# A retention and mixture-of-experts block: the loop written out, row-tiled scores and state, routing weights widened by DMA

## What is computed

```
x = x + attn(layernorm(x));  x = x + ffn(layernorm(x))
attn: q, k = rotary(x Wq, x Wk);  scores = (q k^T) * decay_mask (causal, gamma_h^(t-s));  o = scores v
      o_n = o * rsqrt(mean(o^2)) * g_norm_w;   out = (o_n * silu(x Wg)) Wo
ffn:  comb = top-2 weights of softmax(x gate_w), renormalized
      h_e = silu(x up_w[e] + up_b[e]);  y = sum_e comb_e * (h_e down_w[e] + down_b[e]) + shared expert
```

## Time and profile before

| | |
|---|---|
| Median of 3 runs | 172.55 us (172.54 to 173.57) |
| Profiled execution | 173.23 us, of which span 171.5 us |
| PE busy | 157.3 us (92%) |
| DVE busy | 122.6 us (71%) |
| ACT busy | 82.1 us (48%) |
| POOL busy | 52.9 us (31%) |

### The profile page before, as it was taken

How to read it: one execution, slowest core, us unless ns; L and a number is a source line. 1 busy time by engine, 2 the same in 40 slices (tenths; PEclk the granted TensorE clock), 3 DMA queues, 4 the chain that set the end, 5 groups by cost and what they waited for, 6 DMA issues and landing times.

```text
span 171.5 us, 3275 instructions
## 1 busy us (share of the span) xinstructions
PE 157.3 (92%) x1072; PEld 112.7 (66%) x1072; DVE 122.6 (71%) x350; ACT 82.1 (48%) x155; POOL 52.9 (31%) x73
## 2 busy tenths in 40 slices
PE   6499988989899999999999999999999999999981
PEld 6399665848668777556877865666678656564430
DVE  3759899798898988773789977865678665744411
ACT  3142772334399535232697617024897522973110
POOL 8799418460633340400060611100606111000000
PEclk9999999999999999999999999999999999999999
DMA  4960000000000000000100000000200000010002
GB/s 156 332 214 0 0 4 2 4 0 0 0 6 2 2 0 4 0 0 4 33 28 0 0 0 0 0 0 0 61 2 0 4 0 0 0 48 15 0 0 61
DMA packets 5568, 4.21 MB, mean 25 GB/s; under 512 B 794, under 2 KB 5172, under 8 KB 5556
## 3 DMA queue, kind: packets, MB, share of 16 engines
q1 hardware_dynamic: 5140, 3.53, 6.9%
q10 hardware_dynamic: 416, 0.52, 0.8%
HBM read 3.01 MB, written 1.05 MB: 24 GB/s over the span
## 4 chain that ended last, share of the span: by engine, by line
PE 71%; DVE 14%; issue 6%; POOL 3%; ACT 3%; DMA 2%; DVEq 0%; POOLq 0%; ACTq 0%
PE bY L1192 17%; PE bS L1072 6%; PE bC L1179 5%; PE bU L250 5%; PE bU L252 4%; PE bU L251 4%; PE bV L1131 4%; PE bO L1108 3%; PE bY L996 2%; DVE XN L664 2%; PE bO L1102 2%; PE bV L1122 2%; PE bV L250 2%; PE bX L1053 2%; DMA X<-x 2%
## 5 line engine op out<-in xcount | busy, mean ns | idle before, releaser
L1192 PE MATMUL bY<-HG,DW 128*128 128x512 f32 x64 | 31.6, 593 | 0.0
L356 POOL TENSOR_TENSOR RR<-MS,NHALF 128x8 f32<-128x8 f32 x8 | 13.6, 1700 | 56.5 <-DVE MS L735 56.5
L502 ACT ACTIVATE HB<-bU,UB 128x512 f32<-128x512 f32 x36 | 24.4, 690 | 13.2 <-PE bU L252 12.7
L832 DVE TENSOR_TENSOR HG<-bC,HB 128x512 f32<-128x512 f32 x32 | 22.1, 691 | 11.7 <-PE bC L1179 9.3
L250 PE MATMUL bU<-XH,UWH 128*128 128x512 f32 x36 | 18.9, 524 | 0.1
L1179 PE MATMUL bC<-CT,SEL 128*128 128x512 f32 x32 | 16.9, 529 | 1.1 <-DVE HG L832 1.0
L1072 PE MATMUL bS<-QBD,KT 128*128 128x512 f32 x28 | 14.7, 608 | 1.1 <-DVE S L726 0.6
L1192 PEld LDWEIGHTS bY<-HG,DW 128*128 128x128 f32 x64 | 11.6, 190 | 5.2 <-issue 3.8
L375 POOL TENSOR_TENSOR RS<-VE,NHALF 128x2 f32<-128x2 f32 x8 | 6.0, 746 | 28.8 <-DVE VE L764 28.7
L252 PE MATMUL bU<-XH,UWL 128*128 128x512 f32 x36 | 14.2, 395 | 0.0
L251 PE MATMUL bU<-XL,UWH 128*128 128x512 f32 x36 | 14.1, 392 | 0.0
(11 more groups left out here) (151 smaller groups left out, 351.8 us busy)
## 6 DMA issues: line engine op xcount, KB each, us to landing
out<-OUT SPq DMA_DIRECT2D x8, 128.0 KB, 1.9
X<-x SPq DMA_DIRECT2D x7, 128.0 KB, 4.9
UW<-upw SPq DMA_DIRECT2D x1, 576.0 KB, 5.8
DW<-dnw SPq DMA_DIRECT2D x1, 576.0 KB, 6.3
W<-wqkvg ACTq DMA_DIRECT2D x1, 384.0 KB, 4.0
CN<-const SPq DMA_DIRECT2D x1, 228.5 KB, 3.3
X<-x ACTq DMA_DIRECT2D x1, 128.0 KB, 2.8
WO<-wot SPq DMA_DIRECT2D x1, 128.0 KB, 6.0
```

The source lines that it names most:

```text
L356: pool.tensor_tensor(RR[:, p], MS[:, p], NHALF[:, 0:2 * H], ALU.pow).then_inc(rr.sem, 1)
L502: act.activation(HB[:, k, :], bU[k % 2][:, :], ACT.Silu, bias=UB[:, e:e + 1]).then_inc(hid.sem, 1)
L832: dve.tensor_tensor(HG[:, k % RING, :], bC[:, :], HB[:, k, :], ALU.mult).then_inc(gated.sem, 1)
L1192: pe.matmul(bY[:, :], DW[:, w], HB[:, 0, :] if k == 0 else HG[:, k % RING, :], start=(k == 0), stop=(k == E)).then_inc(down.sem, 1)
```

## The change

- **Order.** The loop is gone; every step of the four groups is written out, and each engine has an order of its own. PE's order also has explicit waits (`after(signal, ...)`) where a bank must be free. The groups' attention runs further ahead of the experts: the first up projection comes after the scores of pair (1, 1) and after the projections of group 2's first pair.
- **Scores and state.** Queries and keys are copied once, to QKT. Scores are 8 matmuls for a pair, each on 32 rows (one head) and 128 columns, each head into its own bank of bA (four banks). S holds only the 32 x 64 block of each head, one head in each strip of 32 partitions; attend's state part is 8 matmuls of 32 rows and 64 columns, the update one DVE instruction. masked works on a pair with two instructions of 512 elements, as before one for each tile.
- **Banks.** q/k, v, gates and the transposed q/k have one bank of bA each; x1_t, state_add, out_t, proj_out, x2_t, router and comb_t share the bank bM.
- **Routing weights.** For groups 0 to 2 the 8 rows of comb go from a copy in SBUF (CR) to a scratch in memory, and four DMAs (two experts each) write them to all partitions (CB); gating reads CB. The last group keeps spread_comb, now into two banks of bA in turn.
- **Moved.** Normalizing (from group 1 on, and all of the second layernorm) from DVE to ACT with a bias computed on DVE; eps additions, the low parts of the expert weights, the output norm's folding and the selector's copy from DVE to POOL. Rotary tables are loaded (4 x 512 KB) instead of built on POOL. keep_x1 is gone, the sum is written to X itself. keep_busy counts 23 instead of 30.
- **Routing.** Ranks are taken on logits, and the softmax's division is left to the last renormalization.

```diff
-            def scores(g, m):
...
-                pe.matmul(score_bank(g, m)[:, :], KT[:, p, b, :], QBD[:, p, b].rearrange("r h n -> r (h n)"), start=True,
-                          stop=True).then_inc(sc_ps.sem, 1)
+            def scores(g, p):
+                pe.wait_ge(qkt.sem, qkt.at(g, p))
                 for b in range(2):
                     for h in range(H):
                         r = slice(h * DK, (h + 1) * DK)
+                        last = pe.matmul(bA[:, h, b * P:(b + 1) * P], QKT[r, p, 1, b, :], QKT[r, p, 0, b, :], start=True,
+                                         stop=True)
+                last.then_inc(sc_ps.sem, 1)
...
+            def attend(g, p):
...
-                        pe.matmul(bO[:, b * HV:(b + 1) * HV], QT[:, p, b, :], S[:, p, b, :], start=(b == 0), stop=False)
+                            pe.matmul(bA[:, h, b * DV:(b + 1) * DV], QKT[r, p, 0, b, :], S[r, n % 4, b * DV:(b + 1) * DV],
+                                      start=(b == 0), stop=False)
...
-                pe.matmul(bC[:, :], SEL[:, expert(k), :], CT[:, :], start=True, stop=True).then_inc(spread.sem, 1)
+                if k <= 2:
+                    pe.wait_ge(ogr.sem, ogr.at(LAST, 1))
                 else:
+                    pe.wait_ge(gated.sem, gated.at(LAST, k - 3))
+                pe.matmul(bA[:, k % 2, :], SEL[0:EX0, expert(k), :], CT[0:EX0, LAST % 2, :], start=True,
+                          stop=True).then_inc(spread.sem, 1)
...
+            def widen(g):
+
+                sp.wait_ge(cr_sb.sem, cr_sb.at(g))
+                sp.dma_start(scratch[g], CR[EX0:EX0 + E, :]).then_inc(sent.sem, 16)
+                sp.wait_ge(sent.sem, 16 * (g + 1))
+                for j in range(E // 2):
+                    if g:
+                        sp.wait_ge(gated.sem, gated.at(g - 1, 2 * j + 1))
+                    src = scratch[g, 2 * j:2 * j + 2, :].unsqueeze(0).to_broadcast([P, 2, GC])
+                    sp.dma_start(CB[:, 2 * j:2 * j + 2, :], src).then_inc(wide[j].sem, 16)
...
             def gating(g, k):
+                if g == LAST:
+                    dve.wait_ge(spread.sem, k)
+                    src = bA[:, k % 2, :]
+                else:
+                    if k % 2:
+                        dve.wait_ge(wide[(k - 1) // 2].sem, 16 * (g + 1))
+                    src = CB[:, k - 1, :]
...
-                for h in range(H):
-                    r, c = slice(h * DK, (h + 1) * DK), slice(h * DV, (h + 1) * DV)
-                    last = dve.scalar_tensor_tensor(
...
+                dve.scalar_tensor_tensor(out=S[:, (n + 1) % 4], in0=S[:, n % 4], scalar=CN[:, GCH0:GCH0 + 1],
+                                         in1=bM[:, 0:2 * DV], op0=ALU.mult, op1=ALU.add).then_inc(st.sem, 1)
...
             keep_busy(10)
             x1_t(0)
-            keep_busy(4)
+            keep_busy(8)
             proj_qk(0, 0)
-            keep_busy(8)
+            proj_g(0, 0)
+            proj_qk(0, 1)
             proj_v(0, 0)
+            after(xl1, 0)
+            x1_t(1)
+            proj_v(0, 1)
```

More of the change, by code:

```diff
@@ L1212, in _ @@
             scores(0, 0)
[L1213 to L1224 removed]
+            after(xl1, 1)
+            state_add(0, 0)
+            keep_busy(3)
+            attend(0, 0)
+            after(st, 0, 0)
+            state_add(0, 1)
@@ L1375, in _ @@
-            y_t(g)
+            after(x1, 0, 0)
+            state_add(1, 0)
+            after(ogr, 0, 1)
+            scores(1, 0)
+            after(st, 1, 0)
+            x2_t(0, 0)
+            attend(1, 0)
+            after(xl2, 0, 0)
+            out_t(0, 1)
+            proj_out(0, 1)
+            after(ogr, 1, 0)
+            proj_qk(2, 0)
+            after(ogr, 1, 0)
+            proj_v(1, 1)
+            after(ogr, 1, 0)
+            proj_g(1, 1)
+            after(ogr, 1, 0)
+            qk_t(1, 1)
@@ new lines, in _ @@
+            scores(1, 1)
+            up_proj(0, 0)
+            after(ogt, 1, 0)
+            x1_t(3)
+            up_proj(0, 1)
+            attend(1, 1)
+            after(xl1, 3)
+            state_add(2, 0)
+            up_proj(0, 2)
+            after(st, 2, 0)
+            router(0)
+            up_proj(0, 3)
+            after(ogr, 1, 1)
+            scores(2, 0)
+            up_proj(0, 4)
+            after(route_a_step, 0, 0)
+            proj_out(1, 0)
+            up_proj(0, 5)
+            down_proj(0, 0)
@@ new lines, in _ @@
+            after(x1, 1, 0)
+            out_t(1, 1)
+            attend(2, 0)
+            proj_out(1, 1)
+            up_proj(0, 6)
+            up_proj(0, 7)
+            after(x1, 1, 1)
+            x2_t(1, 0)
+            after(ogr, 2, 0)
+            proj_v(2, 1)
+            after(ogr, 2, 0)
+            proj_g(2, 1)
+            after(ogr, 2, 0)
+            proj_qk(3, 0)
+            after(xl2, 1, 0)
+            comb_t(0)
+            up_proj(0, 8)
+            after(ogr, 2, 0)
+            qk_t(2, 1)
@@ new lines, in _ @@
+            y_t(0)
+            up_proj(1, 6)
+            after(v_sb, 3, 1)
+            after(sg, 3, 1)
+            scores(3, 1)
+            after(x1, 2, 1)
+            out_t(3, 0)
+            up_proj(1, 7)
+            down_proj(1, 0)
+            after(ogt, 3, 0)
+            state_add(3, 0)
+            down_proj(1, 1)
+            after(st, 3, 0)
+            x2_t(2, 1)
+            attend(3, 1)
+            down_proj(1, 2)
+            after(xl2, 2, 1)
+            router(2)
+            down_proj(1, 3)
```

1636 lines of the change are left out of this document (815 added, 821 removed).

## The result

The changed kernel takes **154.01 us** (median of 4 runs, 153.01 to 155.38), against 172.56 us for the kernel before; the ratio is 0.8898, 95% interval 0.8854 to 0.8943. 156 was predicted, with 150 to 166 as the range. A few executions, such as the one of 155.38 here and two of the four of wide_moved, ran in a slower state at a lower granted clock; medians and ranges count them, ratios do not.

The account below looks back on a forecast made before the run. The prediction took a VectorE-set lead, then TensorE's instruction stream, as the bound. Lead 48.5, filled part 103.3 and end 3.5 sum to a 155.3 us span; with 1.05 added, 156.3, say 156 us, range 150 to 166.

Parts of the forecast that it names:

- Lead: Start to first up projection: first projection at 11.45, 31 us of VectorE work, 6 idle; 48.5 us against 47.87 before.
- Scores' packs: A pair's eight score matmuls on row tiles: 0.5 us instead of 1.72, saving 1.22 a pair, 2.44 a group.
- State's packs: A pair's eight state matmuls in attend, on row tiles: 0.45 us instead of 0.86, saving 0.82 a group.
- The row shows none of a cost: TensorE, state matmuls to half-width ones: changing tile shape priced at nothing, against some tenths of a microsecond a pair by rule.
- Spreads: 24 of 32 routing-weight spreads leave TensorE at 0.23 us each: 1.84 us saved a group, for three groups.
- Widening: DMAs spreading routing weights between comb_t and gating: first takes 3.6 us including start, with 4.9 us left for it.
- Gating from SBUF: Gating on VectorE with two SBUF inputs: 0.708 us against 0.691 before, so nothing gained there.
- Filled part: First up projection to last sum: 93.9 us of TensorE work times a factor of 1.10, 103.3 us.
- Tiles without overlap: Rival for score and state matmuls: row tiles do not overlap, 172.6 us, or 164 at half overlap; chance 0.12.
- Clock in the lead: Rival: TensorE at half rate through the lead's middle, +5 us, 161, or the whole lead, +10, 166; chance 0.10.
- Shared banks: Rival: shared banks stall the filled part, factor 1.2 instead of 1.1, 9.4 us more, 166; chance 0.08.
- Late weights: Rival: widened weights reach gating late, 160 us, or 194 at 60 GB/s; chance 0.08, 0.03 of it slower than before.

Follow-up runs that it names:

- wide_moved: Kernel before plus only the DMA widening of routing weights, with VectorE's statistics, rotation and normalization of a token pair moved ahead of gated products 1 and 2; 180.82 us.
- pool_order: Changed kernel with GpSimd's selector moved behind the fourth group's deviation and the first attention output's normalization; 152.91 us, ratio 0.8866.
- full_scores: Changed kernel with each score matmul contracting all 128 rows instead of its head's 32; 162.15 us, ratio 0.9382.
- spread_time: Changed kernel with 24 512-column float32r matmuls put back on TensorE, one for each spread taken away; 157.62 us, ratio 0.9097.
- wide_late: Changed kernel with each group's widening DMAs held back by two 576 KB loads on the same queue; 177.89 us, ratio 1.0284.
- before_wide: Kernel before with only the DMA widening of routing weights added and 24 spreads gone, in its own orders; 190.38 us, ratio 1.1014.
- full_state: Changed kernel with attend's state matmuls contracting all 128 rows instead of 32; 166.26 us, ratio 0.9609.
- norm2_dve: Changed kernel with the second normalization back from ScalarE to VectorE; 153.39 us, ratio 0.8903.
- both: Changed kernel with the edits of norm2_dve and pool_order together; 153.92 us, ratio 0.8931.
- less_busy: Changed kernel without the 13 filler matmuls behind the first transposes and in the lead, the first ten kept; 156.2 us, ratio 0.8992.

## Why the prediction was right, step by step

The mechanism is the predicted one: row tiles overlap, TensorE's own work bounds the filled part, and the span is 3.3 us under the 155.3 that was summed. Of the signs that were named, "DVE near 103 us", the first up projection near 48.5 and no stretch at 0.21 behind 20 us came; records 23 to 35 ns apart did not (38 and 41), and a gated product did wait for CB, twice, 1.5 us in all.

- **Lead.** 48.5 predicted, 48.42 measured; that they agree so closely is luck. Its terms erred in both directions: VectorE was busy 29.4 us in it, not 31, and stood 7.5, not 6. And the first projection, taken over at 11.45, comes at 11.4 or at 10.2 from one execution to another (pool_order).
- **Scores' packs.** 0.5 predicted between the bounds 0.37 and 1.76; 0.66. **State's packs:** 0.45 predicted; 0.60. The direction was right (full_scores: 111 ns a record against 41), the terms were 0.15 too small: four row tiles overlap less well than the column tiles they were priced by (23 ns). The gain of a pack in scores is 1.06, not 1.22, and 0.86 where the way back costs 0.2.
- **"The row shows none of a cost" for changing the tile shape: wrong.** The step looked at one row, from the state matmuls to the half-width ones. The rows where it shows are the full-width matmuls behind narrow tiles, 0.43 instead of 0.23 in the chain above, and with full_scores it is gone. The kernel before had them too, behind state_add (four transposes in 0.65 instead of 0.44 us, at 45.72). The rule of the Trainium skill (TensorEngine Tiling (Array Packing), section Tiling Modes), that a change of the mode drains the engine, agrees with these rows.
- **Spreads.** 1.84 a group predicted; in spread_time two thirds of such work came back as time.
- **Widening.** 3.6 us for the first transfer predicted; 4.1 to 8.1 us from issue to landing, the median 6.3, and slices of up to 357 GB/s, so every partition reading the same rows is no slower than the loads. The gate waited 1.5 us in all, as said hidden. But its price as a rival was far too low. It was given "a few late microseconds ... (160)"; wide_late shows 24 us for 7 us of delay a group, and before_wide 18 us slower than before with no delay at all. The prediction priced a late transfer by the down projection that needs it and did not ask what stands behind the waiting gate in VectorE's queue. What made the widening nearly free (0.8 us) was the other part of the change, the order, as far as wide_moved shows it.
- **Gating from SBUF.** 0.708 predicted for two SBUF inputs; 0.683, no difference from a bank. The 0.708 of the earlier trace rows is a mean with one long instruction in it (0.831 us, the median is 0.688).
- **Filled part.** 93.9 x 1.10 = 103.3 predicted; 100.1, a factor of 1.07 as in the kernel before. The work was 93.9 + 4 x 0.16 + 5 x 0.15 for the packs + some 4 x 0.2 for the scores' returns = 96.1, and TensorE stood 1.3 us up to 145. The remaining 2.7 us were not traced step by step; the 0.34 behind the router is one of them. The expected growth of the factor by shared banks did not come: the 3 us by which the prediction was too high lie here. The same sum says what the gain is made of: TensorE's work in this part fell from 112.4 to 96.1 us, 16.3, while the part itself fell by 20.1. The other 3.8 us are waits and lengthened steps that are gone. They go with the new orders and banks; no run has these alone, so that share is argued, not shown.
- **End.** 3.5 predicted and measured. **VectorE** 103 predicted, 101.0; **ScalarE** about 80, 84.1.
- **The rivals.** Tiles without overlap: refuted by full_scores. Clock in the lead: behind 12 us it did not fall in the changed kernel's two profiles, but in full_state, norm2_dve and both it did, at 35 to 47 us, and less_busy has it up to 15.6 us. This rival was near: full_state's gaps are the changed kernel's own, norm2_dve has one of 1.6 instead of 1.1 us. From the first projection to the first up projection these kernels take 1.9 (less_busy), 2.2 (both) and 3.0 us (norm2_dve) more, and full_state 6.9, of which its two longer packs at full rate are 2.3. So the fall cost some 2 to 4.6 us where 5 was the price. Shared banks: no sign. Late weights: not here, and dearer than priced.

## What to carry to other kernels

A wait for a DMA on an in-order engine costs what is queued behind it, on that engine and on those that wait for that work, and behind all six stalls of TensorE of about 5 us (before_wide, wide_late) a stretch at half rate followed, behind those of about 3 us (wide_moved) in two of three. So move a transfer under cover together with the order around the wait: the same widening lost 18 us in the old order, 6 with a few steps of that order moved, and 0.8 us in the new kernel. Thin contractions gained by row tiles: eight float32 matmuls of 32 rows (16 records) took 0.66 us instead of 1.78 on all rows, and up to 0.2 us went to the way back to full width. And look at more than one profile of a kernel before a microsecond is put down to an edit.

## What the hardware showed that was not expected

VectorE instructions with two tensors in SBUF, and GpSimd's multiply OG (two tensors in SBUF too), exclude each other in this trace. Timelines of both engines in the changed kernel, VectorE first:

```profile
25.56 1.58 DVE L666 TENSOR_TENSOR QKR<-RA,RB 128x512 f32<-128x512 f32 x1
```
```profile
84.22 0.68 DVE L795 TENSOR_TENSOR HG<-CB,HB 128x512 f32<-128x512 f32 x1
84.82 1.00 DVE L724 SCALAR_TENSOR_TENSOR NM<-MV,RS 128x2 f32<-128x2 f32 x1
```
```profile
25.55 1.04 POOL L323 TENSOR_TENSOR OG<-OGR,RR 128x512 f32<-128x512 f32 x1
```
```profile
84.21 1.59 POOL L323 TENSOR_TENSOR OG<-OGR,RR 128x512 f32<-128x512 f32 x1
```

At 25.6 us OG had begun first, keeps its 1.04, and QKR, usually 0.68, ends 0.55 us behind it. At 84.2 it is the reverse: the gated product keeps its 0.68, OG takes 1.59 instead of 1.04 and ends 0.9 later, and NM behind it, two numbers a partition and usually 0.16, takes 1.00 and ends with OG. Products that read a bank kept their time beside an OG (RA at 91.07 took 0.69). In all there are five such meetings in the trace (25.6, 43.2, 65.5, 84.2 and 105.3 us), which lengthen six instructions by 0.55 to 0.9 us each. It is read from the trace alone; no run was made for it. The Trainium skill (SBUF — State Buffer, section SBUF: two separate sides) states that the two engines share a pair of ports under an exclusive lock, held for a whole instruction, which the one that starts first gets; these rows agree.

The other surprise is how little idle time it takes for the clock to fall in the lead: with full_state two waits of 1.1 us were followed by some 10 us at 1.2 GHz, while the changed kernel, with waits of 1.1 at the same places but shorter work between, stayed at 2.4 GHz. In the changed kernel itself the four transposes at 7.6 us took 1.12 us and in pool_order's the same four 0.66, behind waits of 1.3 and 1.5. What decided it is open; no run here was made for it.
